# A selective scan with 32 channels by 4 states on the partitions, its state sum in four column strips of TensorE, and a new order of the node steps

## What is computed

```
# Mamba: I = 512 channels, N = 16 states, per sequence of L = 128 steps
dt  = softplus(rmsnorm(x_dbl[..., :R]) @ dt_proj_w.T + dt_proj_b)
dA  = exp(dt[..., None] * A)                   # A = -exp(A_log), I x N
dBu = (dt * u)[..., None] * Bm[:, :, None, :]
h   = dA_t * h + dBu_t                         # scan over the steps
y   = einsum('lbin,bln->bli', h_seq, Cm)       # sum over the 16 states
y   = (y + u * D) * silu(gate);  out = y @ out_proj_w.T

# graph: node c reads earlier nodes' outputs
q, k, v = edges of earlier nodes, through Wq, Wk, Wv (8 heads of 32)
node[c] = act_w * (softmax(q k^T / sqrt(32)) v @ Wo + edge(q source))
```

## Time and profile before

| what | value |
|---|---|
| median of the runs | 1480.11 us |
| the profiled execution | 1485.58 us, of which the span is 1483.8 us |
| PE busy, DVE busy, ACT busy | 1285.7, 1070.5, 728.0 us |
| PE busy, DVE busy, share of the span | 87%, 72% |
| mean granted TensorE clock | 0.918 of full speed |
| moved by DMA | 59.35 MB |

### The profile page before, as it was taken

One profiled execution on the slowest core, in us unless ns is written; L12 is line 12 of the kernel. 1 busy time (PEld: TensorE's weight loads), 2 busy tenths in 40 slices (PEclk: granted clock), 3 DMA queues, 4 the chain that ended last, 5 costly groups with the idle time before them and its releaser, 6 DMA issues. The chain is left out here.

```text
span 1483.8 us, 27925 instructions
## 1 busy us (share of the span) xinstructions
PE 1285.7 (87%) x11504; PEld 1024.9 (69%) x11504; DVE 1070.5 (72%) x1714; ACT 728.0 (49%) x1692; POOL 3.8 (0%) x11
## 2 busy tenths in 40 slices
PE   3677668799999999999999999999999988987776
PEld 2656446577777777777777778777877767766665
DVE  0138997688879987998798979897989778533112
ACT  0143443266546654665466546654565545433333
POOL 1000000000000000000000000000000000000000
PEclk8677867699999999999999999999999999987898
DMA  6231310101001100201010102010201020000000
GB/s 205 76 113 64 114 58 8 38 28 54 13 20 60 37 30 16 65 24 43 16 65 10 58 8 73 9 51 8 69 6 58 8 65 8 1 1 8 2 1 8
DMA packets 42047, 59.35 MB, mean 40 GB/s; under 512 B 12032, under 2 KB 18816, under 8 KB 41792
## 3 DMA queue, kind: packets, MB, share of 16 engines
q1 hardware_dynamic: 41920, 57.57, 12.0%
HBM read 55.19 MB, written 2.36 MB: 39 GB/s over the span
## 5 line engine op out<-in xcount | busy, mean ns | idle before, releaser
L942 DVE TENSOR_TENSOR_SCAN unit_buf<-dec,unit_buf 128x512 f32<-128x512 f32 x256 | 311.9, 1218 | 36.4 <-ACT dec L716 36.2
L459 PE MATMUL ps<-unit_buf,cst 128*128 128x256 f32 x1024 | 296.8, 426 | 36.0 <-DVE unit_buf L952 17.4
L459 PEld LDWEIGHTS ps<-unit_buf,cst 128*128 128x128 f32 x1024 | 204.0, 210 | 86.3 <-DVE unit_buf L952 25.4
L716 ACT ACTIVATE dec<-dt,a_neg 128x254 f32<-128x254 f32 x512 | 225.5, 499 | 43.9 <-DVE unit_buf L942 39.1
L934 DVE TENSOR_TENSOR unit_buf<-hs_pad,bs 128x512 f32<-128x512 f32 x256 | 175.1, 686 | 10.8 <-DVE fb L865 0.4
L952 DVE TENSOR_TENSOR unit_buf<-unit_buf,cs 128x512 f32<-128x512 f32 x256 | 175.1, 684 | 0.3
L1056 DVE TENSOR_REDUCE mx<-heads 128x16 f32<-128x2048 f32 x48 | 109.8, 2287 | 81.5 <-PE heads L568 81.5
L788 ACT ACTIVATE pr<-heads 128x512 f32<-128x512 f32 x192 | 99.1, 602 | 50.7 <-PE heads L581 50.7
L528 PE MATMUL ps<-node,wq_f 128*128 128x256 f32 x384 | 94.1, 388 | 9.6 <-ACT node L803 8.7
L604 PE MATMUL heads<-node,we_f 128*128 128x256 f32 x384 | 96.4, 395 | 0.0
L528 PE MATMUL heads<-node,wk_f 128*128 128x256 f32 x384 | 91.8, 382 | 0.0
(11 more groups left out here) (175 smaller groups left out, 1759.1 us busy)
## 6 DMA issues: line engine op xcount, KB each, us to landing
bs<-bc_rows SPq DMA_DIRECT2D x64, 256.0 KB, 3.4
cs<-bc_rows SPq DMA_DIRECT2D x64, 256.0 KB, 3.2
node<-in_w_edgeT SPq DMA_DIRECT2D x18, 256.0 KB, 3.0
xin<-in_x SPq DMA_DIRECT2D x8, 256.0 KB, 2.6
vaug<-in_ctx_in SPq DMA_DIRECT2D x16, 128.0 KB, 2.9
xr<-in_x SPq DMA_DIRECT2D x8, 256.0 KB, 4.3
out_dram<-aT SPq DMA_DIRECT2D x8, 256.0 KB, 4.0
node<-in_w_edge SPq DMA_DIRECT2D x6, 256.0 KB, 4.1
```

Of the source, the lines that this page charges most:

```text
L459: last = mm(MY[:, 0:T], ident, prd[(i * UNITS + k) % PRDS][:, a, :], start=(q == 0 and a == 0), stop=(q == PAIRS - 1 and a == 1))
L716: last = fn(dec[k % 2][:, a, :, 1:L], dt[i % 2][:, c, :].rearrange("p (b t) -> p b t", b=GB)[:, :, 1:L], ACT.Exp, scale=a_neg[:, c * NS + ...
L942: v.tensor_tensor_scan(hst[k % 2][:].rearrange("p a b -> p (a b)"), dec[k % 2][:].rearrange("p a b t -> p (a b t)"), inf[k % 2][:].rearran ...
```

## The change

Three things are changed. First, the layout of the scan: the partitions of a unit hold 32 channels by 4 states (`SN` = 4, `SD` = 32), and the row of 512 elements holds two blocks of 32 channels. A chunk of 128 channels is 4 blocks by 4 groups of states, 8 units, all done before the next chunk. Now dt and dt * u have to be copied to four groups of partitions: `mamba_in` step 10 stores them to DRAM (eight stores of 128 KB), and a new step `chunk` loads each chunk back four times over (512 KB each for dt and for dtu), into two buffers of each, `dts` and `dtus`. B and C need one load of 128 KB for each group of 4 states. `a_neg` is laid out to match by sixteen small loads ahead of the weights. The sum over the states is now partly over partitions: `add` multiplies by `strip` (128 x 32, which adds the four states of a channel), in four column strips of 32, once for two units. `gather` comes up four times in a group instead of eight. `dt` and `hs_pad` have one buffer instead of two, and dtu is kept in `th`.

Second, the node order: edge, node out, keys, queries, where it was edge, keys, node out, queries; `queries` waits for each half of `node_ready` by itself, and `node_max` for each half of the queries.

Third, all slots are new. The steps of `prep`, of which seven stood ahead of group 0's first step, now all come after it.

```
-                *(("f", "attend", _c * STEPS + s) for s in range(STEPS)), ("f", "edge", _c)]
+                *(("f", "attend", _c * STEPS + s) for s in range(STEPS)), ("f", "edge", _c), ("f", "node", _c)]
     if _c + 1 < NODES:
         F_STEPS += [("f", "k", _c + 1)]
-    F_STEPS += [("f", "node", _c)]
...
-P_AT = [-885, -882, -651, -544, -458, -352, -186, -154, -143, -124, -103, -97, -88, -87, -75, -28, -25, -16]
+P_AT = [-122, -122, -122, -107, -101, -100, -90, -86, -82, -65, -64, -45, -42, -41, -34, -14, -6, -1]
...
+                if step == 10:
+                    after(sp, "dt_ready", i, 1)
+                    for k in range(BLKS):
+                        sp.dma_start(dt_rows[i % 2, 0, :, :, k, :].rearrange("c d t -> d c t"),
+                                     dt[k * SD:(k + 1) * SD, :, :]).then_inc(sig["dt_stored"], 16)
+                    after(sp, "dtu_ready", i, 1)
...
+            def chunk(i, c):
+                for j, (dst, name, used) in enumerate(((dts, "dt", "decay"), (dtus, "dtu", "inflow"))):
+                    after(sp, f"{name}_stored", i, 16 * BLKS)
+                    after(sp, used, i, (c - 1) * CUNITS)
+                    sp.dma_start(dst[c % 2][:].rearrange("p k t -> p (k t)"),
+                                 dt_rows[i % 2, j, c].rearrange("d k t -> d (k t)").partition_broadcast(SN)
+                                 ).then_inc(sig[f"{name}_in{c % 2}"], 16)
...
+            for n in range(SN):
+                for k in range(BLKS):
+                    load(a_neg[n * SD:(n + 1) * SD, :, k, :],
+                         vecs[k * SD:(k + 1) * SD, V_ALOG:V_ALOG + IC * NS].rearrange(
+                             "d (c n g) -> n d c g", c=IC, n=SN)[n], "alog_loaded")
             load(win[:], w_in, "win_loaded")
...
-            def add(i, k):
-                m, q = k // PAIRS, k % PAIRS
+            def add(i, j):
+                c, q = j // NGRP, j % NGRP
                 if q == 0:
-                    after(pe, "y_read", i, m)
-                after(pe, "outflow", i, k + 1)
-                for a in range(2):
-                    last = mm(MY[:, 0:T], ident, prd[(i * UNITS + k) % PRDS][:, a, :],
-                              start=(q == 0 and a == 0), stop=(q == PAIRS - 1 and a == 1))
+                    after(pe, "y_read", i, c)
+                after(pe, "outflow", i, 2 * j + 2)
+                for k in (2 * j, 2 * j + 1):
+                    for a in range(2):
+                        r0 = SD * (k % 2 * 2 + a)
+                        last = mm(MY[r0:r0 + SD, 0:T], strip[:], prd[(i * UNITS + k) % PRDS][:, a, :],
+                                  start=(q == 0), stop=(q == NGRP - 1), tile_position=(0, r0))
...
             def feed(i, k):
-                hf, c, q = k // (UNITS // 2), k // PAIRS % IC, k % PAIRS
-                after(dve, f"bs_in{q}", i, 16 * (hf + 1))
-                if k == 0:
-                    after(dve, "dtu_ready", i, 1)
+                c, q, pair = k // CUNITS, k % CUNITS // 2, k % 2
+                if k % CUNITS == 0:
+                    after(dve, f"dtu_in{c % 2}", i, 16 * (c // 2 + 1))
+                if c == 0 and pair == 0:
+                    after(dve, f"bs_in{q}", i, 16)
...
-            def gather(i, m):
+            def gather(i, c):
                 uc = u[i % 2][:, c, :]
-                after(dve, "ysum", i, (m + 1) * PAIRS)
-                if m >= IC:
-                    after(dve, "y_read", i, c + 1)
-                src = MY[:, 0:T]
-                if hf == 0:
-                    v.scalar_tensor_tensor(uc, uc, col(V_D + c), src, ALU.mult, ALU.add).then_inc(sig["y_read"], 1)
-                else:
-                    v.tensor_tensor(uc, uc, src, ALU.add).then_inc(sig["y_read"], 1)
-                    after(dve, "y_read", i, m + 1)
-                    v.tensor_tensor(gate[i % 2][:, c, :], gate[i % 2][:, c, :], uc, ALU.mult).then_inc(sig["y_ready"], 1)
+                after(dve, "ysum", i, (c + 1) * NGRP)
+                v.scalar_tensor_tensor(uc, uc, col(V_D + c), MY[:, 0:T], ALU.mult, ALU.add).then_inc(sig["y_read"], 1)
+                after(dve, "y_read", i, c + 1)
+                v.tensor_tensor(gate[i % 2][:, c, :], gate[i % 2][:, c, :], uc, ALU.mult).then_inc(sig["y_ready"], 1)
...
             def queries(i, c):
-                if c >= 1:
-                    after(pe, "node_ready", i, c)
-                project(FA, wq_f[c], node[SLOT[GRAPH[c]["q"]]], "q_ps")
+                src = node[SLOT[GRAPH[c]["q"]]]
+                for k in range(HC):
+                    if c >= 1:
+                        after(pe, "node_ready", i, (c - 1) * HC + k + 1)
+                    for a in range(HC):
+                        last = mm(FA[:, a * T:(a + 1) * T], wq_f[c][:, k, a * P:(a + 1) * P], src[:, k, :],
+                                  start=(a == 0 and k == 0), stop=(k == HC - 1), skip_group_check=True)
```

More of the change, by code:

```diff
@@ L64 @@
 A_STEPS = [("a", "in", k) for k in range(11)]
-U_STEPS = []
+U_STEPS = [("u", "bc", 0), ("u", "ch", 0), ("u", "bc", 1), ("u", "ch", 1), ("u", "bc", 2), ("u", "bc", 3)]
 for _k in range(UNITS + 1):
-    if _k == 0:
-        U_STEPS += [("u", "bc", n) for n in range(PAIRS)]
-    if _k < UNITS:
-        U_STEPS += [("u", "unit", _k)]
-    else:
-        U_STEPS += [("u", "last", 0)]
-    if UNITS // 2 - PAIRS <= _k < UNITS // 2:
-        U_STEPS += [("u", "bc", _k - UNITS // 2 + 2 * PAIRS)]
-    if _k % PAIRS == 2 and _k > PAIRS:
-        U_STEPS += [("u", "gather", _k // PAIRS - 1)]
-    if _k >= 2:
-        U_STEPS += [("u", "add", _k - 2)]
-U_STEPS += [("u", "add", UNITS - 1), ("u", "gather", 2 * IC - 1)]
+    U_STEPS += [("u", "unit", _k)] if _k < UNITS else [("u", "last", 0)]
+    if _k % CUNITS == 1 and CUNITS < _k < (IC - 1) * CUNITS:
+        U_STEPS += [("u", "ch", _k // CUNITS + 1)]
+    if _k >= 2 and _k % 2 == 0:
+        U_STEPS += [("u", "add", _k // 2 - 1)]
+        if _k % CUNITS == 0:
+            U_STEPS += [("u", "gather", _k // CUNITS - 1)]
 X_STEPS = [("x", "ml", k) for k in range(5)]
@@ L184, in build @@
         ctxT = sb("ctxT", [P, HC, T])
[L185 removed]
+        hs_pad = sb("hs_pad", [P, IC, GB, L + 3])
         u = [sb(f"u{j}", [P, IC, T]) for j in range(2)]
         gate = [sb(f"gate{j}", [P, IC, T]) for j in range(2)]
[L188 to L189 removed]
+        dt = sb("dt", [P, IC, T])
         th = sb("th", [P, IC, T])
@@ L192, in build @@
         xsq, xrs = th[:, 0, :], th[:, 1, :]
+        dtu = th
         xdn = sb("xdn", [P, T])
-        bs = sb("bs", [P, PAIRS, 2, T])
-        cs = sb("cs", [P, PAIRS, 2, T])
+        bs = sb("bs", [P, NGRP, T])
+        cs = sb("cs", [P, NGRP, T])
+        dts = [sb(f"dts{j}", [P, BLKS, T]) for j in range(2)]
+        dtus = [sb(f"dtus{j}", [P, BLKS, T]) for j in range(2)]
         dec = [sb(f"dec{j}", [P, 2, GB, L]) for j in range(2)]
@@ L365, in _ @@
             load_xr(1)
-            walk(dict(pprep=prep, ain=mamba_in, ubc=spread, xout=mlstm_out, fout=ffn_out))
+            walk(dict(pprep=prep, ain=mamba_in, ubc=spread, uch=chunk, xout=mlstm_out, fout=ffn_out))
             sp.wait_ge(sig["out_stored"], 16 * NG)
@@ L802, in node_out @@
                 for a in range(HC):
-                    last = fn(node[SLOT[c]][:, a, :], X1[:, a * T:(a + 1) * T], ACT.Identity,
-                              bias=fb[:, c, 6 + a:7 + a])
-                last.then_inc(sig["node_ready"], 1)
+                    fn(node[SLOT[c]][:, a, :], X1[:, a * T:(a + 1) * T], ACT.Identity,
+                       bias=fb[:, c, 6 + a:7 + a]).then_inc(sig["node_ready"], 1)
             def ffn_out(i, _):
@@ L1088, in _ @@
             g.memset(ones[:], 1.0)
-            for j in range(2):
-                g.memset(hs_pad[j][:].rearrange("p a b t -> p (a b t)"), 0.0)
+            g.memset(hs_pad[:].rearrange("p a b t -> p (a b t)"), 0.0)
             for j in range(2):
```

136 lines of the change are left out of this document (68 added, 68 removed).

## The result

| | kernel before | changed kernel |
|---|---|---|
| median of the runs, us | 1481.43 (1479.05 to 1483.19) | 1507.43 (1499.26 to 1514.97) |
| profiled span, us | 1483.8 | 1501.5 |
| mean granted TensorE clock | 0.918 | 0.849 |
| moved by DMA, MB | 59.35 | 76.15 |

The ratio of the runs is 1.0165, 95% interval 1.0136 to 1.0193 (the two medians of the table alone give 1.0176): the change made the kernel 1.65% slower, where 7% faster was forecast.

A forecast was written before the change was run, and what follows sets the result against it. PE was taken to set the steady period, DVE right behind. Span: 250 (start) + 150 (group 0) + 5 x 143 + 141 + 118.5 + 3.3 = 1377.8 us, a median of 1374 us; range 1318 to 1435 us.

The forecast's parts named there:

- the 512 KB chunk takes between 3.4 and 6.6 us: 10 to 14 us: Way of dtu through DRAM: eight stores issued, landing, then the chunk load, 10 to 14 us from dtu in all.
- a wait of 0 to 2: DVE at each group's first feed: 12 us of other work covers most of the copy, leaving 0 to 2 us.
- first feed: Group 0's scan start: first feed at 70 to 72 us instead of 110.6, 39 us earlier, including 11 us for copying dt.
- first node input: Start of group 0's nodes: 250 us instead of 289, bounds 235 and 270.
- A granted clock of 0.95 or more: Sign that the forecast is right: PE's granted clock stays at 0.95 or more in the steady windows.
- by the clock: Rival: PE loses its gapless run and clock; at 0.90 the period is 148, span 1413 us; chance 0.05.
- by the copies: Rival: chunk loads come late at all four chunks and DVE stands still, deciding from 15 us per group; chance 0.03.
- Strips: Sum over states on PE: four strips run side by side, 10.2 us per group instead of 28.2, saving 18.0.
- drain for each change of mode: PE's tiling switches: a drain at each would leave the period unmoved from 0.66 us each; the trace's row has 0.16.
- DVE's work: Steady period: four gathers' adds go, 1.6 us per group, so DVE work falls from 132.3 to 130.7 us.
- Moving `prep`: Start: group 0 no longer waits behind two and a half weight foldings; with the copy counted, 39 us earlier.
- the order: Node order: queries 5.2 us behind the edge instead of 6.4, saving 5.5 us in group 7, nothing counted in steady groups.

The follow-up runs named there:

- e9: The changed kernel with only the first B and C load moved ahead of the copies' stores, loads still on four engines; 1487.02 us, ratio 1.0014.
- e2: The changed kernel with each chunk load and each B and C load issued as four loads of 32 partitions; 1453.78 us, ratio 0.9795.
- e7: e2 with the first B and C load of a group asked for ahead of the copies' eight stores; 1410.33 us, ratio 0.9496.
- e15: The changed kernel with four matmuls of constants more in each node, ahead of PE's wait for the maxima; 1478.47 us, ratio 0.9985.
- e5: e2 with the sums over states issued over the whole array again instead of in four strips; 1501.80 us, ratio 1.0119.
- e8: e2 without the stores and chunk loads of dt and dtu, the units reading constant tiles; 1398.34 us, ratio 0.9423.
- e4: The changed kernel with the old slots of prep, seven steps ahead of group 0's first step; 1567.53 us, ratio 1.0549.
- e11: e7 with the old node order, the node output behind the next node's keys; 1430.78 us, ratio 0.9627.
- e10: e7 with the second chunk and the third and fourth B and C load asked for behind the second unit; 1403.82 us, ratio 0.9466.

## Why the prediction was wrong

**The step that failed** is "the 512 KB chunk takes between 3.4 and 6.6 us: 10 to 14 us", and with it "a wait of 0 to 2". In the group shown above, the way from the end of dtu to the request of the chunk took 5.7 us (665.06 to 670.78), under the 7.0 forecast; from the request to the feed it was 15.2 us. Together that is 20.9 us in place of 10 to 14, and the wait was 11.2 us on average. Two things had been put at nothing. The first is the form: both rows are loads described over 128 partitions, and the changed loads ran on four engines. The second is what stands ahead: an estimate from the 104 GB/s of the window from 677 to 683 us gives only 5.0 us for one chunk of 512 KB alone, inside the forecast, but B, C and the chunk of dt, asked for in the 1.8 us before it, bring another 768 KB over the same four engines, 7.6 us more. The runs bear out both: DVE's wait for dtus falls from 89.7 us to 68.5 with the first B and C load earlier (e9), to 29.9 with sixteen engines (e2), and to 3.8 with both (e7).

The same error sat in the start: first feed at 77.6 in place of 71, a wait of 13.0 us there and of 6.7 for the third B load, and the start's loads queued behind each other. e7, without it, has its first feed at 66.3 and its first node input at 257.3 (forecast 250). The two edits of e7 take 10.8 of the 14.3 us off the period and 41.8 of the 47.3 us off the end of group 0.

**The period's second error** was the clock. "A granted clock of 0.95 or more" was expected; it was 0.87 to 0.93. The rival "by the clock" priced 0.90 at a period of 148; e7, at 0.90 to 0.92, has 146.9 to 148.7, and 141.3 at 0.98. So the rival's price held at 0.90; at 0.98 its formula gives 136 where 141.3 was measured, so PE does not set the period alone there. Its chance of 0.05 was too low. On the changed kernel the clock was the smaller part: e15 takes 2.3 us off each period, net of what its filler costs; the loads and their place take 157.3 - 146.5 = 10.8.

**The rival "by the copies"** was asked the wrong question: late at all four chunks, 15 us a group. Only the first chunk was late, by 11.2 us; with the lower clock that was enough to use up the gain.

**What held.** PE's timeline of the changed kernel, one sum and what follows it:
```profile
579.54 0.64 PE L479 MATMUL ps<-unit_buf,strip 128*32 128x256 f32 x8
580.11 0.66 PE L536 MATMUL ps<-vaug,ml_buf 128*128 128x65 f32 x4
```
Strips: the eight instructions and the switch back take 0.57 us, so 16 sums cost 9.1 us against 10.2 forecast, and side by side, as the attention's rows said; e5 prices them at 48 us. No drain for each change of mode shows beyond that. DVE's work was 130 us (130.7). The trace shows no wait of a gather (L986). The first feed without the copy was put at 59 us; e8 has it at 60.5. Moving `prep` is worth 55 us at the first node input in e4, where 39 were forecast. The queries stand 5.9 us behind the edge in group 7 (1387.62 to 1393.54; 5.2 forecast), and the order is worth 4.4 us in that group by e11 (5.5), but I counted nothing for it in the steady groups, where it gives 2.6 each.

**The form of the sum held as well.** With the loads mended, first in the queue and PE's wait filled, the kernel has a period of 143.3 and a span of 1372.9 us; the forecast was 143 and 1377.8. Much of that agreement is luck: the forecast knew no filler, and without it the same kernel (e10) has a period of 144.3 and a span of 1396.7 us. With it the last two groups are 14 us shorter than forecast, and group 0 ends 7 us later.

## What to carry to other kernels

Price a transfer by a row of the same description, not of the same bytes: look at the slowest dimension of source and target, and at the DMA share while it runs; here the share sat at a quarter, and it was four engines. When a load moves onto a chain, add up what stands ahead of it in its queue; one place was worth 43 us here once the loads were fast, and 20 us before. When a change takes work off PE, read the granted clock behind its longest waits: part of the gain can be lost there. Matmuls of constants inside the wait, no longer than the wait, brought the clock back here.
